# Attention and MLP layer on one core: score operands projected into stacked fp32r pieces on chip, units worked off in halves, exponential moved behind the transposes, longer lags

## The reference

```python
xn = layernorm(x)
# attention: norms xn again, times ln_g plus ln_b, 16 heads of 8 features
q, k, v = (xn2 @ Wq + bq), (xn2 @ Wk + bk), (xn2 @ Wv + bv)
p = (pe @ Wp)                                   # sinusoidal positions, the same for all batches
content = einsum("bihd,bjhd->bhij", q + u_bias, k)
pos = relative_shift(einsum("bihd,jhd->bhij", q + v_bias, p))
attn = softmax((content + pos) * scale)         # 512 x 512 for each batch and head
out = (attn @ v) @ Wo + bo
# ffn: [x, -x] -> 512 -> 512 -> 128 with weights of +1 and -1, relu times 2 between
```

## Time and profile before

| | |
|---|---|
| runs | 1977.56, 1988.16, 1987.92 us; median 1987.92 |
| span of the profiled execution | 1977.2 us; its own time isn't stated apart, the median of the runs stands 10.7 us above this span |
| busy | PE 1926.8 (97%), ACT 1480.0 (75%), DVE 1456.3 (74%), POOL 603.2 (31%) |
| DMA | 598.90 MB, mean 303 GB/s |
| mean granted TensorE clock | 0.997 |

### The profile page before, as it was taken

How to read it: one execution, slowest core, us unless ns; L and a number is a source line. 1 busy time by engine, 2 the same in 40 slices (tenths; PEclk the granted TensorE clock), 3 DMA queues, 4 the chain that set the end, 5 groups by cost and what they waited for, 6 DMA issues and landing times.

```text
span 1977.2 us, 44868 instructions
## 1 busy us (share of the span) xinstructions
PE 1926.8 (97%) x15684; PEld 866.1 (44%) x15684; DVE 1456.3 (74%) x3510; ACT 1480.0 (75%) x3299; POOL 603.2 (31%) x675
## 2 busy tenths in 40 slices
PE   5999999999999999999999999999999999999996
PEld 1344444444444444444444444444444444444443
DVE  5477777777777777777777777777777777777876
ACT  3687777777777777787777777777777777877773
POOL 5433323242232422333233232332333233131100
PEclk9999999999999999999999999999999999999998
DMA  4899998989989999998999989899999999989993
GB/s 142 295 304 319 300 326 306 315 298 321 319 308 314 305 320 306 316 324 294 310 302 328 317 303 325 292 322 317 307 320 308 309 316 307 316 305 311 318 327 124
DMA packets 117640, 598.90 MB, mean 303 GB/s; under 512 B 16364, under 2 KB 38940, under 8 KB 51880
## 3 DMA queue, kind: packets, MB, share of 16 engines
q1 hardware_dynamic: 117416, 596.03, 90.9%
HBM read 304.80 MB, written 291.16 MB: 301 GB/s over the span
## 4 chain that ended last, share of the span: by engine, by line
PE 92%; ACT 2%; DVE 2%; DMA 2%; issue 1%; SPq 0%; POOL 0%; DVEq 0%; ACTq 0%; POOLq 0%
PE ps_pt L712 29%; PE ps_av L726 16%; PE ps_pos L694 16%; PE ps_job L667 13%; PE ps_con L703 11%; PE ps_job L630 2%; PE ps_job L654 1%; PE ps_job L648 1%; PE ps_job L640 1%; DMA shift<-pos_sb 1%; PE ps_job L635 1%; ACT z_t L472 1%; PE ps_job L633 1%; ACT sc_sb L503 1%; PE ps_job L628 1%
## 5 line engine op out<-in xcount | busy, mean ns | idle before, releaser
L591 DVE CUSTOM_DVE_ANT_0 sc_sb<-ps_con,sc_sb 128x512 f32<-128x512 f32 x1024 | 705.6, 689 | 488.8 <-PE ps_con L703 487.0
L503 ACT ACTIVATE sc_sb<-sc_sb,nmax 128x512 f32<-128x512 f32 x1024 | 740.9, 723 | 224.3 <-DVE nmax L591 221.5
L498 ACT COPY pos_sb<-ps_pos 128x512 f32<-128x512 f32 x1024 | 592.5, 579 | 228.7 <-PE ps_pos L694 143.0
L601 DVE COPY pt_sb<-ps_pt 128x512 f32<-128x512 f32 x1024 | 702.3, 686 | 1.9 <-PE ps_pt L712 1.9
L712 PE MATMUL ps_pt<-c_sb,sc_sb 128*128 128x128 f32 x4096 | 672.6, 287 | 0.5 <-DVE pt_sb L601 0.5
L712 PEld LDWEIGHTS ps_pt<-c_sb,sc_sb 128*128 128x128 f32 x4096 | 429.3, 141 | 431.8 <-DVE pt_sb L601 198.0
L726 PE MATMUL ps_av<-pt_sb,v_sb 128*8 128x128 f32 x8192 | 415.1, 275 | 0.5 <-DVE pt_sb L601 0.3
L694 PE MATMUL ps_pos<-stack_p,stack_q 51*128 51x512 bf16 x1024 | 398.5, 392 | 5.2 <-DMA stack_q<-pieces_q 3.2
L703 PE MATMUL ps_con<-stack_k,stack_q 51*128 51x512 bf16 x1024 | 387.5, 378 | 0.2 <-DVE nmax L591 0.2
L430 POOL CAST h<-act_sb 128x512 fp32r<-128x512 f32 x128 | 78.1, 610 | 981.9 <-ACT act_sb L482 981.9
L694 PEld LDWEIGHTS ps_pos<-stack_p,stack_q 51*128 51x128 bf16 x1024 | 94.5, 93 | 304.2 <-issue 219.9
(11 more groups left out here) (87 smaller groups left out, 792.3 us busy)
## 6 DMA issues: line engine op xcount, KB each, us to landing
shift<-pos_sb SPq DMA_DIRECT2D x256, 1026.0 KB, 8.1
sc_sb<-shift SPq DMA_DIRECT2D x256, 1024.0 KB, 8.7
pieces_q<-pieces_sb_q SPq DMA_DIRECT2D x32, 192.0 KB, 5.3
stack_q<-pieces_q SPq DMA_DIRECT2D x64, 96.0 KB
pieces_k<-pieces_sb_k SPq DMA_DIRECT2D x32, 192.0 KB, 5.4
stack_k<-pieces_k SPq DMA_DIRECT2D x64, 96.0 KB
x_sb<-in_x SPq DMA_DIRECT2D x16, 256.0 KB, 7.2
stack_q<-pieces_q SPq DMA_DIRECT2D x64, 64.0 KB
```

The costliest lines, as they stand in the source:

```text
L498: act.copy(pos_sb[:, u % N_POS, t, 0:S], ps_pos[:, t % 2, :]).then_inc(s_pe, 1)
L503: act.activation(sc_sb[:, m % N_SC, t, :], sc_sb[:, m % N_SC, t, :], ACT.Exp, bias=nmax[:, m % N_SC, t:t + 1], scale=-1.0, accum_out=sums[ ...
L591: dve.tensor_tensor_reduce(sc_sb[:, m % N_SC, t, :], ps_con[:, t % 2, :], sc_sb[:, m % N_SC, t, :], -SCALE, BIG, ALU.add, ALU.min, nmax[:, ...
L601: dve.tensor_copy(pt_sb[:, q % N_PT], ps_pt[:, j % 2, :]).then_inc(s_te, 1)
```

## The change

- **Stacks on chip.** Wq, Wk and Wp come from the host spread over 512 columns: for each head three copies of its 8 columns and room for bias rows, 32 columns a head. Jobs QG, KG, PG (c = 0 to 3) each give four heads as 128 rows. ACT evicts them, POOL turns them in two operations into fp32r pieces: some rows keep the rounded value, some the rest. A head's operand is 26 rows (24 for three products, 2 for the bias) from partition `32 * (h % 4)`. P, Q, K, UK, VP, the pieces in DRAM and their DMAs go.
- **Halves.** Each stage is done two quarters at a time: ACT copies 1024 columns of positions at once, PE makes eight transposes and then sixteen value matmul records, a job is done in one piece or in two.
- **Exponential behind the transposes.** DVE subtracts the row's extreme in `sc_sb` (L479), PE transposes, and ACT takes the exponential from `ps_pt` into `pt_sb` (L388), where DVE's copy stood. The row sums come from a ninth column of ones in v; they go with the heads through DRAM and come back with eight more DMAs; DVE takes 128 x 512 reciprocals (L490). INV goes.
- **Lags.** `SHIFT_LAG` 3, `CONTENT_LAG` 6, turn 15 halves and values 16 halves behind positions; one more buffer or two each for `pos_sb`, `sc_sb`, `shift` and `act_sb`. The zero of the pad is written in front of a row, so that the read of `shift` begins at S.

```diff
-    SHIFT_LAG = 2
-    CONTENT_LAG = 4
...
+    SHIFT_LAG = 3
+    CONTENT_LAG = 6
+    TURN_H = 2 * CONTENT_LAG + 3
+    VALUES_H = TURN_H + 1
+    HEADS_SLOT = CONTENT_LAG + 3
     N_X = 4
-    N_POS = 2
-    N_SC = 5
-    N_SHIFT = 4
+    N_POS = 3
+    N_SC = 6
+    N_SHIFT = 6
     N_PT = 4
-
+    N_ACT = 3
...
+        THIS = ((0, "L1", 0, 2), (3, "KG", 1), (4, "QG", 2), (5, "L1", 1, 2), (7, "KG", 2), (8, "L1", 2, 2),
+                (12, "QG", 3), (13, "L1", 3, 2), (15, "KG", 3), (30, "L2", 0, 2))
+        NEXT = ((2, "T1", 0), (17, "TZ", 0), (18, "L0", 0), (20, "QG", 0), (21, "L0", 1), (22, "V", 0),
+                (23, "KG", 0), (24, "L0", 2), (25, "L0", 3), (29, "QG", 1))
...
-                    sp.dma_start(o_t[:, :], heads_d.rearrange("p t c -> p (t c)")).then_inc(s_hr, 16)
...
+                    sp.dma_start(o_t[:, :], heads_d[0:P].rearrange("p t c -> p (t c)")).then_inc(s_hr, 16)
+                    for d in range(DH):
+                        sp.dma_start(sums_t[H * d:H * d + H, :],
+                                     heads_d[P:P + H].rearrange("p t c -> p (t c)")).then_inc(s_hr, 16)
...
+                    if b > 0:
+                        pool.wait_ge(s_con, NT * (H * (b - 1) + GROUP * (c + 1)))
+                    own(pool.tensor_tensor(dst, src, low.broadcast_to([P, S]), ALU.mult))
+                    pool.tensor_tensor(dst, src, dst.bitcast(F32), ALU.subtract).then_inc(s_hl, 1)
+                    pool.wait_ge(s_hl, k + 1)
+                    pool.sem_inc(ready, 1)
...
-                        act.copy(pos_sb[:, u % N_POS, t, 0:S], ps_pos[:, t % 2, :]).then_inc(s_pe, 1)
-                    if m is not None:
-                        act.wait_ge(s_ttr, NT * m + t + 1)
-                        b, h = divmod(m, H)
-                        wait(act, s_inv, b - 1)
-                        act.activation(sc_sb[:, m % N_SC, t, :], sc_sb[:, m % N_SC, t, :], ACT.Exp,
-                                       bias=nmax[:, m % N_SC, t:t + 1], scale=-1.0,
-                                       accum_out=sums[:, b % 2, t, h:h + 1]).then_inc(s_exp, 1)
...
+                    act.copy(pos_sb[:, u % N_POS, 2 * i:2 * i + 2, 1:PITCH], ps_pos[:, :, :]).then_inc(s_pe, 1)
...
+                    act.wait_ge(s_pt, k + 1)
+                    if k == 0:
+                        act.wait_ge(s_wf, 1)
+                    wait(act, s_av, k - 1)
+                    act.activation(pt_sb[:, 2 * i:2 * i + 2, :], ps_pt[:, :, :], ACT.Exp, scale=-1.0) \
+                       .then_inc(s_exp, 1)
...
-                        dve.tensor_copy(pt_sb[:, q % N_PT], ps_pt[:, j % 2, :]).then_inc(s_te, 1)
...
+                    for t in (2 * i, 2 * i + 1):
+                        dve.wait_ge(s_ttr, NT * m + t + 1)
+                        dve.tensor_scalar(sc_sb[:, m % N_SC, t, :], sc_sb[:, m % N_SC, t, :],
+                                          nmax[:, m % N_SC, t:t + 1], None, ALU.subtract).then_inc(s_sub, 1)
...
+                if it >= 1 and h % 32 == NORMAL_HALF:
+                    dve.wait_ge(s_hr, 16 * (DH + 1) * it)
+                    own(dve.reciprocal(sums_t[:, :], sums_t[:, :]))
+                    dve.tensor_tensor(o_t[:, :], o_t[:, :], sums_t[:, :], ALU.mult).then_inc(s_norm, 1)
...
             def at(u):
                 h = u % H
-                base = 64 * (h % 2)
-                return slice(base, base + KR), h // 2
+                base = 32 * (h % GROUP)
+                return slice(base, base + ROWS), h // GROUP
...
-                wait(pe, s_pe, NT * u + t - 1)
-                pe.matmul(ps_pos[:, t % 2, :], QQ[rows, q, t * P:(t + 1) * P], PP[rows, q, :],
-                          start=True, stop=True).then_inc(s_pos, 1)
...
+                if t % 2 == 0:
+                    wait(pe, s_pe, 2 * u + t // 2)
+                ins = pe.matmul(ps_pos[:, t % 2, :], QS[rows, g, t * P:(t + 1) * P], PS[rows, g, :],
+                                start=True, stop=True)
+                if t % 2 == 1:
+                    ins.then_inc(s_pos, 1)
...
-            def turn(u, j):
-
-                if j == 0:
-                    pe.wait_ge(s_exp, NT * (u + 1))
-                wait(pe, s_te, NT * u + j - 1)
-                for t in range(NT):
-                    last = pe.transpose(ps_pt[:, j % 2, t * P:(t + 1) * P],
-                                        sc_sb[:, u % N_SC, t, j * P:(j + 1) * P], id_sb)
+            def turn(u, i):
+                if i == 0:
+                    pe.wait_ge(s_sub, NT * (u + 1))
+                wait(pe, s_exp, 2 * u + i)
+                for j in (2 * i, 2 * i + 1):
+                    for t in range(NT):
+                        last = pe.transpose(ps_pt[:, j % 2, t * P:(t + 1) * P],
+                                            sc_sb[:, u % N_SC, t, j * P:(j + 1) * P], id_sb)
                 last.then_inc(s_pt, 1)
...
+                pe.wait_ge(s_exp, 2 * u + i + 1)
+                for j in (2 * i, 2 * i + 1):
+                    for t in range(NT):
+                        last = pe.matmul(ps_av[32 * t:32 * t + DH + 1, h % 4, :], v_sb[:, b % 2, j, h, :],
+                                         pt_sb[:, j, t * P:(t + 1) * P], start=(j == 0), stop=(j == NT - 1))
...
+            for half in HALVES:
+                u, i = half_of(half, 0)
+                m, k = half_of(half, 2 * CONTENT_LAG)
+                for t in range(2):
                     if u is not None:
-                        positions(u, t)
+                        positions(u, 2 * i + t)
                     if m is not None:
-                        content(m, t)
-                    p, j = block_of(n, t, TURN_Q)
-                    if p is not None:
-                        turn(p, j)
-                    o, j = block_of(n, t, VALUES_Q)
-                    if o is not None:
-                        values(o, j)
-                    for j, part, many in parts(n, t):
-                        do_job(*j, part, many)
-
-
-BIG = 3.4e38
+                        content(m, 2 * k + t)
+                u, i = half_of(half, TURN_H)
+                if u is not None:
+                    turn(u, i)
+                u, i = half_of(half, VALUES_H)
+                if u is not None:
+                    values(u, i)
+                for j in parts(half):
+                    do_job(*j)
```

More of the change, by code:

```diff
@@ L219, in attention_mlp @@
[L219 to L236 removed]
+        ORDER = []
@@ new lines, in attention_mlp, with add @@
+        AT = {}
+        def add(half, name, b, c=0, many=1):
+            AT.setdefault(half, []).append((name, b, c, 0, many))
+            for i in range(1, many):
+                AT.setdefault(half + i, []).append((name, b, c, i, many))
+        START = ((0, "TZ", 0), (1, "QG", 0), (2, "PG", 0), (3, "KG", 0))
+        FIRST = ((0, "T1", 0), (0, "V", 0), (1, "QG", 1), (2, "PG", 1), (3, "KG", 1), (4, "QG", 2), (5, "PG", 2),
+                 (6, "L0", 0), (7, "KG", 2), (8, "L0", 1), (9, "L0", 2), (10, "L0", 3), (11, "PG", 3),
+                 (12, "QG", 3), (13, "L1", 0), (14, "L1", 1), (15, "KG", 3), (18, "L1", 2), (19, "L1", 3),
+                 (29, "L2", 0, 2))
@@ new lines, in attention_mlp @@
+        for half, name, c in START:
+            add(half - 32, name, 0, c)
+        for it in range(B + 1):
+            for b, todo in ((it - 1, LAST), (it, THIS if it else FIRST), (it + 1, NEXT if it else FIRST_NEXT)):
+                for half, name, c, *many in todo if 0 <= b < B else ():
+                    add(32 * it + half, name, b, c, *many)
+        HALVES = range(-32, 2 * UNITS + 32)
+        STEPS = range(-16, UNITS + 16)
+        for h in HALVES:
+            ORDER += [j[:3] for j in AT.get(h, []) if j[3] == j[4] - 1]
@@ L370, in _ @@
+                if it >= 2 and slot == 1:
+                    sp.wait_ge(s_jev, job("TY", it - 2))
+                    sp.dma_start(out[it - 2].rearrange("(p t) d -> p t d", t=NT),
+                                 x_sb[:, (it - 2) % N_X]).then_inc(s_out, 16)
+                if 0 <= it and it + 2 < B and slot == 4:
+                    load_x(it + 2)
                 if it >= 1 and slot == HEADS_SLOT:
@@ L678, in do_job @@
                     last = todo[i]()
-                if first < end == len(todo):
+                if end == len(todo):
                     last.then_inc(s_job, 1)
```

513 lines of the change are left out of this document (203 added, 310 removed).

## The result

| | before | after |
|---|---|---|
| runs, us | 1977.56, 1988.16, 1987.92, 1991.13 | 1821.08, 1811.81, 1805.43, 1802.0 |
| median | 1988.04 | 1808.62 |
| ratio | | 0.9114, 95% interval 0.9067 to 0.9161 |
| profiled execution | | 1821.08, span 1819.3 |

A few executions of the kernel before took over 1.5% longer than its fastest on the same chip; all ratios leave them out, so a ratio isn't exactly that of two medians.

What follows compares the result with a forecast made beforehand. PE's stream was taken as the bound: 71.7 + 30.3 = 102.0 us a batch, 105.3 with DVE's 1.8 and 1.5. 140 + 1474 + 95 + 57 = 1766, with the median's 10.7 1777, said as 1780; range 1705 to 1970.

Steps and rivals of the forecast that it cites:

- The bound and the main loop: PE's own instruction stream is the clock; a half takes 2.24 us (before 2.92), 32 halves 71.7 us.
- the end without overlap: PE's half if positions and content run one by one: 2.70 us, 32 halves 86.4 us.
- The jobs: PE's small jobs beside the main loop: + 4.3 us, so 30.3 us a batch.
- The subtraction: DVE's subtraction from SBUF to SBUF in place of the copy: 0.49 us, with an expected wait for POOL of 0.27.
- The five halves without a job: DVE with some port waits is slower there than PE's 2.24 us: + 1.8 us a batch.
- The reciprocal: DVE's reciprocal of 512 columns, 3.2 to 4.3 us, waits for nine DMAs and delays content: + 1.5 us a batch.
- The rest of the sum: Outside the inner batches: 140 us to the second batch, 95 for the last, tail 57.
- No overlap: Rival: fp32r matmuls on PE do not overlap, 117.5 us a batch, 1966 us (1935 to 1985); chance 0.17.
- The port: Rival: each DVE subtraction waits 0.97 us for POOL, a batch 138 us, the time 2290; chance 0.11.
- a sign of being wrong: The forecast counts as wrong if PE's waits exceed some 5 us a batch.
- The DMA as a bound: Rival: DMA or DVE binds in between; DMA 108 or 112 us a batch, 1815 and 1870 us; chance 0.14.

Runs made afterwards that it cites:

- run 1: Changed kernel with content matmuls taking their rows from the row group of the positions of the same half: 2035.8 us, ratio 1.028 to the kernel before.
- run 4: Changed kernel with the reciprocal of the sums over 64 of 512 columns alone, output not attention's there: 1729.6 us, ratio 0.874 to the kernel before.
- run 7: Changed kernel with a second, contiguous copy of z, written by ACT, for the Q jobs: 1796.8 us, ratio 0.901 to the kernel before.
- run 6: Changed kernel with heads' transfers one step earlier, reciprocal and product in three pieces, output job at half 28: 1776.5 us, ratio 0.891 to the kernel before.
- run 8: Changed kernel with the edits of run 6 and run 7 together: 1778.6 us, ratio 0.891 to the kernel before.
- run 12: run 11 with the second layer norm's statistics at half 20 and three pieces of 80, 80 and 352 columns: 1788.9 us, ratio 0.891 to the kernel before.
- run 5: Changed kernel with the transfers of heads and sums one unit step earlier (`HEADS_SLOT` 8 for 9): 1809.6 us, ratio 0.907 to the kernel before.
- run 10: Changed kernel with the 64-column reciprocal of run 4 and the contiguous z of run 7: 1712.7 us, ratio 0.864 to the kernel before.
- run 11: Changed kernel with reciprocal and product in five pieces, sums read by one transfer, heads' transfers at slot 8, output job at half 28: 1775.5 us, ratio 0.895.
- run 2: Changed kernel with the order position, position, content, content in a half: 1814.0 us, ratio 0.916 to the kernel before.
- run 3: Changed kernel with PE's part alone back in quarters, semaphores still at the half: 2168.1 us, ratio 1.095 to the kernel before.
- run 9: Changed kernel with `SHIFT_LAG` 2 for 3 and `CONTENT_LAG` 5 for 6, `HEADS_SLOT` kept: 1808.3 us, ratio 0.912 to the kernel before.

## Why the prediction was right, and where it was off

**The bound and the main loop: right.** PE's stream is the clock. (Before, thirteen of the fourteen inner batches are 119.4 us and one is 120.0, not all the same to a hundredth; it changes nothing.) Half 2.24 us (measured 2.24 to 2.27), pair 0.66, turn 1.03, values 0.55, the end without overlap 2.70 (measured 2.70 in run 1). The deciding inference was that two positions of different units side by side, in bf16 and 51 rows high, stand for fp32r and 26 rows.

**The jobs: right.** 30.3 us; the batch of 101.8 in run 4, against 102.0, has them in it. Q's four strided jobs cost 0.9 us each over contiguous ones, as run 7 shows.

**The subtraction: right, with the mixture unlike the mean.** The median is 0.482 us (said 0.49), 219 of the 1024 take over 1.1 and up to 1.6 us, each beside a POOL operation with two operands in SBUF (L319, L328), so the mean is 0.687: a port wait of 0.21 where I said 0.27, far from the 0.68 from which that rival decides. The five halves without a job, for which I added 1.8 us a batch, are not longer at all: DVE falls behind in them and makes it up in the next.

**The reciprocal: the term that was too small.** "Content two halves later needs its buffer: + 1.5 us" names the right wait. Its price is 6.8 us a batch (108.6 less 101.8), 5.7 of them gone with the short reciprocal (mean 102.9). Two things were left out. DVE was already behind: in batch 8 it works without a pause from 955.9 us to the reciprocal at 971.2, so nearly all of the 3.3 + 0.7 us came on top, and PE stood still for 2.6 us even where the sums were in time, 3.1 on average. And the granted clock: 7.1 us at 1.2 GHz behind it, on average, cost half of that. Together 6.6 of the 6.8. 14 x (108.6 - 105.3) is 46 us of the 53 by which the span of 1819.3 lies over 1766.

**The rest of the sum.** First batch 132.9 (said 140), last 104.3 (95), tail 62.0 (57). The span is 53 us over its sum, but the median only 29 over the forecast, and that is luck: the median, 10.7 us above the span before, is 10.7 below it after, which makes 21 of the difference, and the rounding up to 1780 is the rest.

**The rivals.** No overlap: 2035.8 us in run 1, where I gave 1966; the stall with its half clock is in it as well. The port: three of its signs came, batches that vary, PE waiting for DVE at content, and subtractions over 0.5 us (mean 0.687). They didn't single it out. Run 4 has the same subtractions (mean 0.688), and with the short reciprocal alone PE's waits for DVE are 4.9 us. The port has a part in DVE's backlog, though: in batch 8 the last two pairs of subtractions ahead of the reciprocal take 1.54 and 1.37 us, where an undisturbed pair takes 0.88. PE's idle time of some 3 us a batch stayed under the 5 us that I had named as a sign of being wrong, a sign that doesn't count the clock behind the wait. The DMA as a bound is not reached by the changed kernel (share 0.97 to 0.99), but it is the next one, as transfers that land late and not as bytes.

What makes them late in runs 6, 8 and 12 is shown in part. The slot of the heads' transfers has a share in it: run 5, with slot 8 and the stall still in place, has 37.5 us of ACT's wait for a write of `shift`, the changed kernel, with slot 9, 4.7. At slot 8 SP waits for the eviction of the heads in every batch (53.2 us in run 5, only once in the changed kernel), with the read of `shift` queued behind it. That PE's stall is gone isn't enough by itself: run 4 has slot 9 and batches of 102.9 us on average, and 3.8 us of this wait. A quicker PE adds to it: runs 7 and 10, with slot 9 and the contiguous z, have 27.8 and 23.7 us. What is left open is why run 11 has only 13.0 us, with slot 8 and 59.0 us of SP's wait, and run 12, which differs from it in the pieces on DVE and in one slot of DVE's and POOL's and ran on another chip, 113.2. Slot 9 with the reciprocal in pieces wasn't tried.

**The parts of the change.** The overlap carries 222 us (runs 1 and 2, on one chip), where the whole change gains 179. PE in quarters, without the longer cover for the exponential, would lose more than that again (run 3). The last unit of the lags gives nothing measurable (run 9); that content stands 6 units behind and not 4 is what puts it in another row group than positions. The exponential behind the transposes takes DVE's copy away and brings the long reciprocal, and with it the only new stall of the changed kernel.

## What to carry to other kernels

Look for pairs of matmuls of few rows and place their operands in different row groups: here that is worth more than the whole gain. Then price every long instruction on the second busiest engine by what stands behind it in its order, and a stall of TensorE by the clock it loses afterwards: 3.1 us idle cost 6.8 on average, and in run 11 stalls of 0.7 us were enough to bring the lower clock. And when a stall has gone, expect what it covered (here the transfers) to become the next one, before counting on the sum.

## What the runs showed of the hardware

- Matmuls of different row groups need not be neighbours in the program: the third in order started 8 ns after the first and 0.33 us ahead of the second (run 2).
- fp32r matmuls of 26 rows overlap in pairs as fully as bf16 ones: 3 ns between starts, and not at all in one row group (0.23 to 0.24 us).
- A reciprocal of 512 columns takes 3.35 us, of 64 columns 0.54: about 6.3 ns for a column, where a subtraction takes 0.9.
- A subtraction of 0.48 us takes up to 1.6 us beside a POOL operation with two operands in SBUF (219 of 1024 over 1.1 us, all of them beside one).
- The granted clock fell to half behind stalls of TensorE of 2.6 to 4.0 us in all fourteen inner batches of the changed kernel, and behind stalls of 0.7 us in most batches of run 11.
- The DMA engines moved 345 and 357 GB/s over two batches of 99.2 us, both at share 1.00, so that share is no measure of what they can still carry; a write of 1026 KB landed after 8.0 us in one schedule and after 15.0 us in another, at nearly the same mean rate (310 and 316 GB/s).
